# A decoder layer on one core: 24 matmuls that nothing reads are left out around the feed-forward products

## The chip, the cores and the metric

The kernel runs on one core of a Trainium2 chip. A core has a matrix engine (TensorE, PE in the profile, with its weight loads as PEld), VectorE (DVE), ScalarE (ACT), GpSimd (POOL) and DMA queues; each engine has its own instruction stream, and the streams meet only at semaphores. The metric is the device time of one execution in microseconds. The kernel before takes 385.61 us (median of 3 runs, 385.21 to 386.19).

## The reference, cut to what matters

A decoder layer in float32 over `x` of 8 x 256 x 128: self-attention of 16 heads of 64, cross-attention to 512 context rows, and a feed-forward layer with quantised products. Only the last part is touched:

```python
x = x + attn(layernorm(x))
x = x + cross_attn(ctx, ctx, layernorm(x))
x = x + ffn(layernorm(x))
def quant_linear(x, w, b):
    xq, s_in = quant_act_uint8(x)      # s_in = max over the WHOLE of x / 255
    wq, s_w = quant_weight_int8_perchannel(w)
    return einsum('btd,fd->btf', xq, wq) + quant_bias_int32(b, s_in, s_w)
h = relu(quant_linear(x, w1, b1))      # 2048 rows: 128 -> 512
return quant_linear(h, w2, b2)         # 2048 rows: 512 -> 128
```

Each of the two quantised layers needs one number, the largest element of its whole input, before its first product can be formed. So all of `h` must be there before the second layer starts.

## The kernel before, in words

Attention runs batch by batch in a loop and takes the span up to about 350 us. TensorE is the busiest engine there. Then the feed-forward layer is done once for all 2048 rows. Its activations stand transposed in `xrT`, 128 x 2048, and are taken in 4 chunks `n` of 512 columns; the hidden layer of 512 is 4 tiles `c` of 128. The order on each engine is written out by hand:

- TensorE, first layer (L726): 16 products `(n, c)`, each a 128x128 f16 weight tile against 512 columns, into the four banks `h_banks[c]` (score0, score1, turned_bank, q_bank1). Product `m` waits until eviction `m - 4` is done, since it takes over that bank (L725).
- ScalarE (L923): 16 evictions with bias and Relu from those banks into `h_sb`, which is part of the tensor `big`.
- VectorE (L1280): 16 reductions, one over each evicted tile, for the maximum. When all are done it forms `fmax`.
- TensorE (`spread_max(1, ...)`, L706): one f32 matmul that turns the 128 partial maxima of `fmax` onto every partition. VectorE then makes the scale out of it (L1239 to L1290).
- VectorE (L1297, 10 tiles) and ScalarE (L759, 6 tiles) quantise `h`; ahead of each tile's product TensorE waits for it (L748: 16 products, four accumulated in each of four banks). ScalarE evicts the four banks (L935), TensorE transposes them back after all 16 products (`turn_back`, L739, 16 transposes), VectorE adds the residual (L1306), and SyncE writes each of the 4 chunks of the output with a DMA of 256 KB.

`keep_warm(count, lhs, rhs, dst)` (L618) issues `count` matmuls into a bank that nothing reads. It is called at five places ahead of these products with the identity matrix, and those calls are not touched. Inside the first layer it is called at three places, with a weight tile and 512 columns of `x_qT` into `side_bank`: once after each product from `m = 4` on (12 matmuls), 8 after the last product, and 4 after `spread_max(1)`. None of these waits for a semaphore or sets one. `side_bank` is written again by the first transposes of `turn_back`.

Of the kernel before, what the change touches and what calls it, by code (L numbers as in the profile page):

```python
# [71 lines left out]
def decoder_layer(nc, x, ctx_in, norm_scale, wq, wk, wv, w_out, b_out, xWk, xWv, xbv, xWq, xbq,  # L72
# [41 lines left out]
    def wait(eng, sem, value):  # L114

        if isinstance(value, int) and value <= 0:
            return
        eng.wait_ge(sem, value)

    with ExitStack() as ctx:  # L120
        def sb(name, shape, dt=F32):
            return ctx.enter_context(nc.sbuf_tensor(name, shape, dt))

        def bank(name):
            return ctx.enter_context(nc.psum_tensor(name, [P, 512], F32))
# [95 lines left out]
        w1_qT = sb("w1_qT", [P, FT, P], F16)  # L221
# [15 lines left out]
        x_qT = xrT[:].bitcast(F16).rearrange("p (t half) -> p t half", half=2)[:, :, 0]  # L237
# [10 lines left out]
        side_bank = bank("side_bank")  # L248
# [201 lines left out]
        def _(pe):  # L450
# [165 lines left out]
            def keep_warm(count, lhs, rhs, dst):  # L616
                for _ in range(count):
                    nc.tensor.matmul(dst, lhs, rhs, start=True, stop=True)  # L618
# [84 lines left out]
            def spread_max(n, dst):  # L703

                pe.wait_ge(fmax_done, n + 1)
                nc.tensor.matmul(dst, fmax[:, n:n + 1].to_broadcast([P, P]), ident[:], start=True, stop=True  # L706
                                 ).then_inc(gmax_raw, 1)
# [11 lines left out]
            for n in range(CHUNKS):  # L719
                pe.wait_ge((xq_even, xq_odd)[n % 2], n // 2 + 1)  # L720
                for c in range(FT):
                    m = n * FT + c
                    if m == 2:
                        pe.wait_ge(xr_done, 5)
                    wait(pe, h_done, m - 3)  # L725
                    nc.tensor.matmul(h_banks[c][:], w1_qT[:, c, :], x_qT[:, n * 512:(n + 1) * 512],  # L726
                                     start=True, stop=True).then_inc(h_raw, 1)
                    if m >= 4:
                        keep_warm(1, w1_qT[:, c, :], x_qT[:, n * 512:(n + 1) * 512], side_bank[:])
            keep_warm(8, w1_qT[:, 0, :], x_qT[:, 0:512], side_bank[:])  # L730
            spread_max(1, acc_bank[:, 2 * P:3 * P])
            keep_warm(4, w1_qT[:, 0, :], x_qT[:, 0:512], side_bank[:])

            pe.wait_ge(h_done, CHUNKS * FT)

# [687 lines left out]
```

## Time and profile before

| | |
|---|---|
| device time, median of 3 runs | 385.61 us (385.21 to 386.19) |
| the profiled execution: device time, span | 386.2 us, 384.4 us |
| TensorE matmuls busy | 370.2 us (96% of the span) |
| VectorE, ScalarE, GpSimd busy | 325.8, 259.6, 174.3 us |
| first layer's products, from the first to the last one's start | 360.04 to 367.62 us |
| second layer's products | 373.43 to 378.34 us |
| transposes back | 378.18 to 380.09 us |

Times in the profile are counted from the span's start. Busy time of an engine is the time in which one of its instructions runs; matmuls overlap their neighbours, so a matmul's recorded duration is longer than its distance to the next one. The granted clock is TensorE's, as a share of 2.4 GHz: 1.00 is 2.4 GHz and 0.50 is 1.2 GHz. In a timeline a row stands for a run of like instructions: start, time from the first's start to the last's end, engine, line, operation, and the count behind the x; what stands in brackets is how long the engine was idle before and who released it.

### The profile page before, as it was taken

What the parts mean: (1) busy time and instruction counts of PE and PEld (TensorE: products, weight loads), DVE (VectorE), ACT (ScalarE), POOL (GpSimd) and SP (SyncE); (2) the same over time, 40 slices, a digit from 0 to 9 for tenths busy, and PEclk for the clock granted to TensorE, in tenths of its full rate; (3) what the DMA queues carried; (4) which work ended last, traced back from release to release, by engine and by line L of the source; (5) the groups of instructions that cost most, each with busy time, mean ns of one, the idle gap of its engine ahead of it and who ended that gap; (6) DMA issues with size and microseconds to landing.
All of it is one profiled execution on the core that took longest, in us unless ns stands there. A gap on an engine that the chain in (4) does not pass through costs nothing.

```text
span 384.4 us, 9135 instructions
## 1 busy us (share of the span) xinstructions
PE 370.2 (96%) x3034; PEld 288.4 (75%) x3034; DVE 325.8 (85%) x790; ACT 259.6 (68%) x812; POOL 174.3 (45%) x188
## 2 busy tenths in 40 slices
PE   8889999999999999999999999999999998999975
PEld 7768778778878877788777888787778876676422
DVE  3888879988998899879998899879987997876995
ACT  3867676766777567766677667756876668725664
POOL 2574435553555445545555454634555543521000
PEclk9999999999999999999999999999999999999999
DMA  7500000001000100001000100000000100000003
GB/s 231 166 15 2 2 0 2 3 3 41 2 1 3 42 0 0 0 0 41 0 0 0 41 0 0 0 30 10 0 0 0 27 2 2 2 2 0 2 0 109
DMA packets 7190, 7.50 MB, mean 20 GB/s; under 512 B 1280, under 2 KB 5120, under 8 KB 7168
## 3 DMA queue, kind: packets, MB, share of 16 engines
q1 hardware_dynamic: 6736, 6.69, 5.6%
q10 hardware_dynamic: 432, 0.52, 0.5%
q8 instruction: 13, 0.21, 0.2%
q14 instruction: 9, 0.07, 0.1%
HBM read 6.16 MB, written 1.05 MB: 19 GB/s over the span
## 4 chain that ended last, share of the span: by engine, by line
PE 81%; DVE 8%; ACT 7%; issue 3%; POOL 1%; POOLq 0%; DVEq 0%; ACTq 0%
PE o_bank L503 15%; PE turned_bank L494 14%; PE score L484 14%; PE acc_bank L510 7%; PE side_bank L453 4%; ACT prob L768 4%; PE q_bank L453 3%; PE q_bank L455 3%; PE q_bank L454 3%; PE side_bank L454 3%; PE side_bank L455 3%; PE side_bank L564 3%; DVE h_max L1280 2%; PE score L618 2%; PE side_bank L557 2%
## 5 line engine op out<-in xcount | busy, mean ns | idle before, releaser
L1324 POOL TENSOR_TENSOR prob<-prob,rinv 128x512 f32<-128x512 f32 x128 | 133.4, 1044 | 156.7 <-DVE rinv L955 156.4
L768 ACT ACTIVATE prob<-score,negmax 128x256 f32<-128x256 f32 x252 | 116.9, 473 | 36.2 <-DVE negmax L951 34.4
L958 DVE COPY pT<-turned_bank 128x512 f32<-128x512 f32 x124 | 84.1, 679 | 12.5 <-PE turned_bank L494 10.9
L951 DVE TENSOR_REDUCE negmax<-score 128x2 f32<-128x512 f32 x126 | 85.8, 682 | 3.4 <-PE score L484 1.1
L494 PE MATMUL turned_bank<-ident,prob 128*128 128x128 f32 x496 | 76.8, 277 | 0.3 <-DVE pT L958 0.2
L503 PE MATMUL o_bank<-pT,v_sb 128*64 128x256 f32 x504 | 68.3, 392 | 0.0
L494 PEld LDWEIGHTS turned_bank<-ident,prob 128*128 128x128 f32 x496 | 56.3, 141 | 9.1 <-issue 0.6
L768 ACT ACTIVATION_READ_ACCUMULATOR prob<-score,negmax 128x1 f32 x252 | 51.4, 204 | 0.0
L943 DVE TENSOR_TENSOR q_lo<-q_bank,q_hi 128x512 fp32r<-128x512 f32 x63 | 43.3, 689 | 6.8 <-ACT q_hi L759 4.9
L484 PE MATMUL score<-q_hi 64*128 64x256 f32 x252 | 42.3, 330 | 3.8 <-ACT prob L768 3.2
L503 PEld LDWEIGHTS o_bank<-pT,v_sb 128*64 128x64 f32 x504 | 30.5, 136 | 19.6 <-issue 9.2
L484 PEld LDWEIGHTS score<-q_hi 64*128 64x128 f32 x252 | 23.9, 184 | 25.8 <-issue 14.5
L453 PE MATMUL q_bank<-ht_hi,wqk_hi 128*128 128x256 f32 x124 | 40.2, 324 | 0.0
L510 PE MATMUL acc_bank<-wo_sb,oT 128*128 128x128 f32 x256 | 39.1, 276 | 0.0
L759 ACT ACTIVATE q_hi<-q_bank 128x512 fp32r<-128x512 f32 x63 | 38.1, 605 | 0.2
L759 ACT ACTIVATE v_sb<-side_bank 128x512 f32<-128x512 f32 x32 | 19.1, 598 | 26.6 <-PE side_bank L455 26.6
L510 PEld LDWEIGHTS acc_bank<-wo_sb,oT 128*128 128x128 f32 x256 | 34.7, 191 | 1.8 <-ACT oT L759 0.4
L484 PE MATMUL score<-q_lo,q_hi 64*128 64x256 f32 x252 | 35.9, 278 | 0.0
L484 PE MATMUL score<-q_hi,q_lo 64*128 64x256 f32 x252 | 35.8, 277 | 0.0
L455 PE MATMUL q_bank<-ht_hi,wqk_lo 128*128 128x256 f32 x124 | 34.9, 281 | 0.0
L454 PE MATMUL q_bank<-ht_lo,wqk_hi 128*128 128x256 f32 x124 | 34.8, 280 | 0.0
L759 ACT ACTIVATE oT<-o_bank 128x256 f32<-128x256 f32 x63 | 24.5, 388 | 6.2 <-PE o_bank L503 5.9
(249 smaller groups left out, 652.9 us busy)
## 6 DMA issues: line engine op xcount, KB each, us to landing
c_sb<-in_ctx_dram SPq DMA_DIRECT2D x8, 256.0 KB, 2.7
x_sb<-in_x_dram SPq DMA_DIRECT2D x8, 128.0 KB, 2.5
out_dram<-xn_all SPq DMA_DIRECT2D x4, 256.0 KB, 2.4
big<-in_L_attn_wk_dram ACTq DMA_DIRECT2D x2, 256.0 KB, 5.1
big<-in_L_attn_wq_dram SPq DMA_DIRECT2D x2, 256.0 KB, 5.6
big<-in_L_attn_wv_dram SPq DMA_DIRECT2D x2, 256.0 KB, 6.2
wo_sb<-in_L_attn_w_out_dram SPq DMA_DIRECT2D x1, 512.0 KB, 7.5
w_sb<-in_L_ffn_w_dram SPq DMA_DIRECT2D x2, 256.0 KB, 4.5
```

The source lines that it names most:

```text
L453: nc.tensor.matmul(dst, lhs_hi, rhs_hi, start=True, stop=False)
L454: nc.tensor.matmul(dst, lhs_hi, rhs_lo, start=False, stop=False)
L455: return nc.tensor.matmul(dst, lhs_lo, rhs_hi, start=False, stop=True)
L484: last = nc.tensor.matmul(banks[r][:, t * S:(t + 1) * S], query[rows, parity, 0, t * P:(t + 1) * P], key[rows, parity, 1, :], start=(n == ...
L494: last = nc.tensor.transpose(bank[:, kt * S + t * P:kt * S + (t + 1) * P], prob[:, slot, t, kt * P:(kt + 1) * P], ident[:])
L503: last = nc.tensor.matmul(bank[r * E:(r + 1) * E, 0:S], v_sb[:, vp, kt, h * E:(h + 1) * E], pT[:, slots[r], kt, :], start=(kt == 0), stop= ...
L510: last = nc.tensor.matmul(acc_bank[:, t * D:(t + 1) * D], oT[:, pair % 2, t * P:(t + 1) * P], wo_sb[:, pair, :], start=(pair == 0 and t == 0),
L759: return nc.scalar.activation(dst, src, ACT.Copy, **kw)
L768: last = nc.scalar.activation(prob[:, slot, t, :], banks[r][:, t * S:(t + 1) * S], ACT.Exp, bias=negmax[:, slot, t:t + 1], scale=1.0, accu ...
L951: nc.vector.tensor_reduce(negmax[:, slot], banks[r][:].rearrange("p (t k) -> p t k", k=S), X_AXIS, ALU.max, negate=True).then_inc(max_done, 1)
L958: nc.vector.tensor_copy(pT[:, slot].rearrange("p k q -> p (k q)"), bank[:]).then_inc(pT_done, 1)
L1324: nc.gpsimd.tensor_tensor(prob[:, slot], prob[:, slot], rinv[:, slot].unsqueeze(2).to_broadcast([P, QT, S]), ALU.mult).then_inc(prob_done, 1)
```

## The change

Three calls of `keep_warm` are deleted, 12 + 8 + 4 = 24 matmuls of 512 columns, each with its weight load. Everything else is as it was; the lines behind the deleted ones have numbers lower by 4.

```diff
                     nc.tensor.matmul(h_banks[c][:], w1_qT[:, c, :], x_qT[:, n * 512:(n + 1) * 512],
                                      start=True, stop=True).then_inc(h_raw, 1)
-                    if m >= 4:
-                        keep_warm(1, w1_qT[:, c, :], x_qT[:, n * 512:(n + 1) * 512], side_bank[:])
-            keep_warm(8, w1_qT[:, 0, :], x_qT[:, 0:512], side_bank[:])
             spread_max(1, acc_bank[:, 2 * P:3 * P])
-            keep_warm(4, w1_qT[:, 0, :], x_qT[:, 0:512], side_bank[:])
 
             pe.wait_ge(h_done, CHUNKS * FT)
```

On TensorE, in the first layer, one chunk of products (score0, score1, turned_bank and q_bank1 are the four banks of `h_banks`, xrT holds the quantised activations, w1_qT the weights):

```order
 L726 MATMUL q_bank1<-xrT,w1_qT 128x512
 L726 MATMUL score0<-xrT,w1_qT 128x512
-L618 MATMUL side_bank<-xrT,w1_qT 128x512
 L726 MATMUL score1<-xrT,w1_qT 128x512
-L618 MATMUL side_bank<-xrT,w1_qT 128x512
 L726 MATMUL turned_bank<-xrT,w1_qT 128x512
-L618 MATMUL side_bank<-xrT,w1_qT 128x512
 L726 MATMUL q_bank1<-xrT,w1_qT 128x512
-L618 MATMUL side_bank<-xrT,w1_qT 128x512
```

From the fifth product on, each product now stands next to the following one, and the wait of that one for its bank comes straight behind it.

On TensorE, between the two layers, before (fmax holds the partial maxima, big the quantised hidden layer; q_bank and o_bank receive the second layer's products):

```order
L726 MATMUL q_bank<-xrT,w_qT 128x512
L618 MATMUL side_bank<-xrT,w_qT 128x512 x9
L706 MATMUL acc_bank<-ident,fmax 128x128
L618 MATMUL side_bank<-xrT,w_qT 128x512 x4
L748 MATMUL q_bank<-big,w_qT 128x512 x4
L748 MATMUL o_bank<-big,w_qT 128x512 x4
```

and the same place in the changed kernel:

```order
L726 MATMUL q_bank<-xrT,w_qT 128x512
L706 MATMUL acc_bank<-ident,fmax 128x128
L744 MATMUL q_bank<-big,w_qT 128x512 x4
L744 MATMUL o_bank<-big,w_qT 128x512 x4
L744 MATMUL turned_bank<-big,w_qT 128x512 x4
```

The nine (the one behind the sixteenth product and the eight) and the four are gone, so that between the last product of the first layer and the first of the second TensorE has a single matmul, that of `spread_max(1)`.

## Rows read from the trace of the kernel before

**Rows 1.** The page's 40 slices: TensorE's granted clock in tenths.
```profile
PEclk9999999999999999999999999999999999999999
```

**Rows 2.** Chain of waits, 350 to 385 us: start, us, what.
```profile
361.24 8.70 DVE h_max L1280 x15
...
371.30 0.50 PE acc_bank L706 x2
...
378.82 1.89 DVE xn_all L1306 x3
380.70 0.60 DVEq L120
```

**Rows 3.** Timeline, first layer, 360 to 371 us, all engines.
```profile
360.52 1.26 ACT L923 ACTIVATE big<-score,b_col 128x512 f32<-128x512 f32 x2 [0.38 <-PE score L726]
...
361.24 9.59 DVE L1280 TENSOR_REDUCE h_max<-big 128x1 f32<-128x512 f32 x16
...
362.42 0.10 PEld L726 LDWEIGHTS turned_bank<-xrT,w_qT 128*128 128x128 f16 x1 [0.46 <-ACT big L923]
...
362.66 0.39 PE L618 MATMUL side_bank<-xrT,w_qT 128*128 128x512 f16 x1
...
369.08 0.80 ACT L923 ACTIVATE big<-q_bank,b_col 128x512 f32<-128x512 f32 x1
```

**Rows 4.** Timeline of PE from 367.6 to 373.5 us, between the layers.
```profile
367.62 0.40 PE L726 MATMUL q_bank<-xrT,w_qT 128*128 128x512 f16 x1
367.86 2.19 PE L618 MATMUL side_bank<-xrT,w_qT 128*128 128x512 f16 x9
371.30 0.49 PE L706 MATMUL acc_bank<-ident,fmax 128*128 128x128 f32 x2 [1.25 <-DVE fmax L1287]
371.62 1.07 PE L618 MATMUL side_bank<-xrT,w_qT 128*128 128x512 f16 x4
373.43 0.39 PE L748 MATMUL q_bank<-big,w_qT 128*128 128x512 f16 x1 [0.74 <-DVE big L1297]
```

**Rows 5.** Timeline, second layer, 373 to 381 us.
```profile
374.58 2.86 DVE L1297 TENSOR_SCALAR big<-big,h_scale 128x512 f32<-128x512 f32 x7
...
375.11 0.10 PEld L748 LDWEIGHTS o_bank<-big,w_qT 128*128 128x128 f16 x1 [0.86 <-DVE big L1297]
...
377.16 1.18 PE L748 MATMUL q_bank<-big,w_qT 128*128 128x512 f16 x4
...
378.62 1.04 PE L739 MATMUL score<-ident,xrT 128*128 128x128 f32 x8
...
379.49 0.60 PE L739 MATMUL acc_bank<-ident,xrT 128*128 128x128 f32 x4
...
380.62 0.68 DVE L1306 TENSOR_TENSOR xn_all<-acc_bank,x_all 128x512 f32<-128x512 f32 x1
```

**Rows 6.** Windows: length, busy of PE, PEld, DVE, ACT, POOL, clock, DMA.
```profile
371.30:373.40 2.10, 1.39 (x6) 0.60 (x6) 1.47 (x7) 0.60 (x1) 0.00 (x0) 1.00 0.00 0
...
380.10:383.00 2.90, 0.00 (x0) 0.00 (x0) 1.20 (x3) 0.00 (x0) 0.00 (x0) 1.00 0.88 297
383.00:384.40 1.40, 0.00 (x0) 0.00 (x0) 0.00 (x0) 0.00 (x0) 0.00 (x0) 0.50 0.38 135
```

**Rows 7.** Line 618 alone, 1.6 to 7.1 us: minimum/median/maximum ns.
```profile
L618 PEld LDWEIGHTS score<-ident x26: 289/333/338, 1.6 to 6.9; 128*128 128x128 f32 x26
L618 PE MATMUL score<-ident x25: 421/421/580, 1.6 to 6.9; 128*128 128x128 f32 x25
```

**Rows 8.** Line 618 in the whole span: minimum/median/maximum ns.
```profile
L618 PEld LDWEIGHTS side_bank<-ident x28: 190/192/192, 355.4 to 359.6; 128*128 128x128 f32 x28
L618 PE MATMUL side_bank<-ident x28: 275/275/275, 355.5 to 359.7; 128*128 128x128 f32 x28
```

**Rows 9.** Timeline, 352 to 384.4 us: identity matmuls at 355 us.
```profile
355.49 2.40 PE L618 MATMUL side_bank<-ident 128*128 128x128 f32 x20
```

**Rows 10.** Timeline of PE, 1.6 to 8.4 us, and the window 1.6 to 7.5.
```profile
1.61 6.66 PE L618 MATMUL score<-ident 128*128 128x128 f32 x32 [1.61 <-POOL ident L1369]
...
1.60:7.50 5.90, 5.89 (x27) 5.90 (x28) 2.69 (x9) 2.54 (x3) 1.93 (x3) 1.00 0.81 250
```

**Rows 11.** The page's list of DMA issues: the output.
```profile
out_dram<-xn_all SPq DMA_DIRECT2D x4, 256.0 KB, 2.4
```

## The prediction

> **What bounds the kernel now.** I read the slices of the page first, for the clock, then the chain of waits over the last 35 us, the timeline there engine by engine, and windows cut where TensorE starts and stops. The slices show 9 throughout, a granted clock of 2.4 GHz up to the end [rows 1]. The chain shows who holds the time around the change. Through the first feed-forward layer it is VectorE, 15 maxima in a row [rows 2]: the 16 start every 0.59 us ((9.59 - 0.68) / 15), while ScalarE's 16 evictions start every 0.571 us ((369.08 - 360.52) / 15) and stay ahead [rows 3]. TensorE is not in the chain there: its weight load for a product sat idle 0.46 us for ScalarE to give back the bank [rows 3]. Then comes a short relay, last maximum, `fmax`, the spreading matmul of TensorE at 371.30, the scale, the first quantised tiles, and then the second layer's products, the transposes and the additions, with TensorE in the chain [rows 2]. After the last addition only the output's DMAs are left.
>
> **What goes, and what it gives back directly.** 24 matmuls of 512 columns at one per 0.225 us ((2.19 - 0.39) / 8, nine in a row) are 5.4 us of TensorE [rows 4]. None of that is on the path:
> - The 12 beside the products stand in time in which TensorE would wait for a bank; the next product starts when ScalarE is done, not when the side matmul is [rows 3]. Gain 0.
> - The 8 behind the last product (nine with its own) end at 370.05; the spreading matmul starts at 371.30, after 1.25 us of idling for `fmax` [rows 4]. Gain 0.
> - The 4 behind it end at 372.69, and the first product of the second layer starts at 373.43 after 0.74 us of idling for a quantised tile [rows 4]. Gain 0.
> - No semaphore hangs on them, so no other engine's waits change.
>
> What could be gained is less contention. ScalarE's evictions grow from about 0.63 to 0.80 us in the record while their distance stays, and VectorE reads only `big` there, so the 0.59 us step of the maxima is the pace to be sped up. Its bounds are 0 and the step falling to ScalarE's 0.571: 15 x 0.023 = 0.35 us. I take 0, since VectorE and TensorE share no tile there.
>
> **What they cover.** With them TensorE's idle stretches between the layers are 1.25 and 0.74 us, and the clock stays at 1.00 [rows 4, 6]. Without them the last product of the first layer ends at 368.0, the spreading matmul comes at 371.30 and runs 0.5 us, and nothing follows till 373.43: 3.3 us idle, one matmul, 1.6 us idle. The nearest row is the end of the program: TensorE's last transpose ends at 380.09, the clock is 1.00 from 380.10 to 383.00 and 0.50 from 383.00 on [rows 5, 6]. So 2.9 us after TensorE stopped the chip took the clock to 1.2 GHz. By the same delay it would fall at 368.0 + 2.9 = 370.9, ahead of the spreading matmul, and the second layer would begin at 1.2 GHz. Even if it held until 371.3, one matmul of half a microsecond in a stretch of 5.4 us is little to keep it up. The Trainium skill, "TensorE: Matmul & The Clock Gate", What's actually happening, says the same from the other side: the slow clock is the default and activity is what lifts it, with no levels but the two. By that rule the side matmuls are work after all; the trace's drop at 383.00 agrees.
>
> **What the slow clock costs.** Its price in matmuls is read where the same form runs at both. The identity matmuls at the start of the program take 421 ns, their weight loads 333 [rows 7]; those at 355 to 360 us take 275 and 192 [rows 8]. The page gives 1.00 for the start too (window 1.60 to 7.50 [rows 10]), but the durations show the lower level: the distance from one to the next is 0.221 us at the start (25 of them from 1.6 to 6.9, 5.3 / 24) against 0.112 us at 355 us ((2.40 - 0.28) / 19) [rows 7, 9]. The ratio is 1.97, so a 512-column product goes from 0.225 to an estimated 0.443 us.
>
> - First layer: if the clock fell already there, a product would take 0.443 us in a step of 0.57, and it has three evictions' time (1.7 us) before ScalarE wants it. Cost 0.
> - Spreading matmul: two passes. Each is 0.146 us longer in latency (421 - 275), overlapping, and the second starts 0.109 us later (0.221 - 0.112): 0.26 us, right on the path. The other end is 0, if the clock falls later than 371.3. I take 0.26, because 370.9 is earlier.
> - Second layer: 16 products now take 373.43 to 378.34, 4.91 us, because they wait for tiles. The last tile of VectorE is ready at 374.58 + 2.86 = 377.44 [rows 5]. At 0.443 us each the products no longer wait for any tile (the fifth would start at 373.43 + 4 x 0.443 = 375.20, and its tile let it start at 375.11 [rows 5]), so TensorE becomes the bound. If the clock is low for t microseconds from the first product on, t / 0.443 products are done in it, the rest follow at 0.225, and the last one's drain is 0.17: t + (16 - t / 0.443) x 0.225 + 0.17 = 3.77 + 0.492 t. Over the 4.91 of now that is 0.492 t - 1.14.
>
> The disputed number is t, how long TensorE must work before the clock comes back. The trace has one such return: from the first matmul at 1.61 until about 7.5 us all are slow [rows 7, 10], 5.9 us of almost unbroken work. The other row on how fast the chip answers is the 2.9 us of the fall [rows 6]. With t = 5.9 the cost is 1.76 us, with 2.9 it is 0.29 us. Neither is nearer, since the one started from a cold chip with a wait for x in the middle and the other is a fall, so I take the middle, t = 4.4, and 0.492 x 4.4 - 1.14 = 1.02 us.
>
> **Where the delay ends up.** The first chunk's transposes follow the last product, the first addition follows them, and each DMA follows an addition, so a delay of the last product reaches the end whole. The additions (0.60 us apart) and the four DMAs keep their pace; the output's transfer, 256 KB four times [rows 11], is busy until about 383 [rows 6]. Sum: 0 + 0.26 + 1.02 = 1.3 us, on the profiled execution 386.2 + 1.3 = 387.5 us. That execution stands 0.6 us above the median of the runs, so the forecast on the median is 385.61 + 1.3 = 386.9 us.
>
> **Rivals.**
> - *The clock never falls* (not slower). The place is 368.0 to 373.4. For it: the fall at 383.00 came after total silence, while here a matmul interrupts at 371.30, and 1.25 and 0.74 us of idling did nothing. Against it: 3.3 us is longer than 2.9. It decides if the silent stretch that the chip bears is over 3.3 us; then the cost is 0 and the time 385.6 us.
> - *The clock falls and does not come back before the end.* The products then take 16 x 0.443 + 0.17 = 7.26 us, 2.35 more. The 16 transposes come at a distance of 0.110 us now ((1.04 - 0.27) / 7 [rows 5]) and of 0.22 then, another 1.75. The last addition starts at 380.62 where its tile was ready at 380.09 [rows 5], so 0.53 of that is absorbed, and the last DMA waits behind the others some 0.5 us now, which goes too. With 0.26 for the spreading matmul the cost is 0.26 + 2.35 + 1.75 - 0.53 - 0.5 = 3.3 us, time 388.9 us. For it: the return took 5.9 us in the one case seen, and the slow products last 7.3. Against it: 5.9 is less than 7.3. The Trainium skill, same page, Part 4: PE-mode transpose, says that the full clock does not engage for transposes. The transposes of this trace run at 1.00 with 0.110 us between them, so they do not lose a clock that is up; whether they could raise one no row here shows, and if not, a clock still low at the last product stays low, which is this rival.
> - *Less contention*: the maxima speed up and the clock stays. 385.61 - 0.35 = 385.3 us, the floor.
>
> **How the numbers follow.** Clock falls and returns during the second layer 0.72, with 385.9 to 387.6 us as its own range (0.29 to 1.76, with 0 to 0.26); never falls 0.13; never returns 0.10; less contention 0.05. A measurement of this kernel tells about 0.3%, 1.16 us, from no change. In the likeliest case that needs 0.492 t - 1.14 + 0.26 over 1.16, t over 4.15, some 58% of 2.9 to 5.9: 0.42. With the 0.10 of no return, slower has 0.52; faster by that much has 0.02, since no mechanism gives over 0.35 us; the rest, 0.46, is the same. The range is 385.5 to 388.3 us: it takes in the unchanged case and a t somewhat past 5.9, and leaves out most of the no-return case.
>
> **What the profile after would show.** The fall: a granted clock of 0.50 in a window between 371 and 377 us, and the 9s of the slices broken near the end. The spreading matmul: its two passes at 0.7 to 0.75 us instead of 0.49. The second layer: its first products 0.44 us apart, the weight loads no longer waiting for VectorE, later ones 0.22 apart, with the change of distance 3 to 6 us behind the first product. First layer: the maxima still 0.59 us apart and over by 370.9. The forecast is wrong if the clock is 1.00 in all windows up to the transposes' end (then no change), if the transposes are 0.22 us apart (then +3.3), or if the first layer gets longer or shorter by over 0.4 us.

## The result, and the profile after

The changed kernel takes 387.82 us (median of 7 runs, 386.3 to 388.3) beside 385.44 us before (385.12 to 386.19). The ratio is 1.0053, 95% interval 1.0036 to 1.0070: about 2.0 us slower (1.4 to 2.7). The two medians lie 2.4 us apart; the ratio goes by all the executions of both, and the sums below are held against its 2.0. Two more sets of runs of the same kernel gave 1.0048 (1.0035 to 1.0061) and 1.0036 (1.0021 to 1.0051).

The page's slices of the changed kernel, which answer to [rows 1]:

```profile
PE   8889999999999999999999999999999998999855
...
PEclk9999999999999999999999999999999999999958
```

Windows of the changed kernel, cut at what TensorE does; columns as in [rows 6]:

```profile
360.00:365.00 5.00, 3.55 (x12) 0.86 (x9) 4.92 (x11) 4.89 (x9) 0.00 (x0) 1.00 0.01 3
365.00:370.90 5.90, 2.72 (x6) 0.45 (x5) 5.75 (x12) 4.47 (x8) 0.00 (x0) 0.50 0.00 0
370.90:373.30 2.40, 0.77 (x2) 0.49 (x3) 1.49 (x7) 0.61 (x1) 0.00 (x0) 0.50 0.00 0
373.30:378.60 5.30, 5.28 (x13) 1.72 (x14) 3.88 (x12) 4.51 (x8) 0.00 (x0) 0.50 0.00 0
378.70:381.30 2.60, 2.60 (x20) 2.00 (x18) 1.23 (x3) 1.50 (x2) 0.00 (x0) 1.00 0.00 0
```

The clock stands at 2.4 GHz up to 365.0, in the middle of the first layer, at 1.2 GHz from there to between 378.6 and 378.7, and at 2.4 GHz again for the transposes. Second layer and the matmul ahead of it, on TensorE, timeline of the changed kernel, where [rows 4, 5] stood:

```profile
367.21 0.61 PE L726 MATMUL q_bank<-xrT,w_qT 128*128 128x512 f16 x1
370.88 0.80 PE L706 MATMUL acc_bank<-ident,fmax 128*128 128x128 f32 x2 [3.06 <-DVE fmax L1283]
373.32 1.86 PE L744 MATMUL q_bank<-big,w_qT 128*128 128x512 f16 x4 [1.65 <-DVE big L1293]
375.00 1.89 PE L744 MATMUL o_bank<-big,w_qT 128*128 128x512 f16 x4
376.69 1.91 PE L744 MATMUL turned_bank<-big,w_qT 128*128 128x512 f16 x4
378.40 1.20 PE L744 MATMUL q_bank<-big,w_qT 128*128 128x512 f16 x4
...
379.87 1.04 PE L735 MATMUL score<-ident,xrT 128*128 128x128 f32 x8
```

Four products take 1.69 us from group to group, 0.42 us each, and nothing stands in brackets behind the second and third group: the tiles are there, TensorE is the bound. The last group is at 2.4 GHz for the most part, 1.20 us against 1.18 in [rows 5]. The spreading matmul takes 0.80 us, not 0.49.

The chain of waits, changed kernel (answers to [rows 2]):

```profile
360.83 8.71 DVE h_max L1276 x15
...
370.88 0.81 PE acc_bank L706 x2
...
373.32 1.86 PE q_bank L744 x4
375.19 1.71 PE o_bank L744 x4
376.89 1.71 PE turned_bank L744 x4
...
380.07 1.89 DVE xn_all L1302 x3
381.95 0.60 DVEq L120
```

The maxima take what they took (8.71 us against 8.70). Three groups of products stand in the chain in a row, 1.86, 1.71 and 1.71 us.

**Where the time went.** Counted from the first product of the first layer (360.04 before, 359.62 after) to the span's end, the kernel before takes 24.36 us and the changed one 26.04, so +1.68 in this pair. Three parts make it up. From the first product to the spreading matmul it is 11.26 us in both, a difference of 0.00. The spreading matmul gives 0.31. The 16 products take 6.28 us (373.32 to 379.60) against 4.91, which gives 1.37. Everything behind is shifted. The profiled span is only 1.3 us longer since the changed kernel reached the first layer 0.42 us earlier, for a reason that has nothing to do with the change (last section).

### The profile page after: what moved, and what is told of

Same layout as the page of the kernel before. It is cut to its first block, busy times and chain, and to the rows that moved or that the text cites. A ratio compares the mean times of both kernels' runs of the same rounds, so it can differ in the third digit from the quotient of the medians.

```text
span 385.7 us, 9087 instructions
## 1 busy us (share of the span) xinstructions
PE 367.8 (95%) x3010; PEld 287.5 (75%) x3010; DVE 325.8 (84%) x790; ACT 260.2 (67%) x812; POOL 174.6 (45%) x188
## 4 chain that ended last, share of the span: by engine, by line
PE 81%; DVE 7%; ACT 7%; issue 3%; POOL 1%; POOLq 0%; DVEq 0%; ACTq 0%
PE o_bank L503 15%; PE turned_bank L494 14%; PE score L484 14%; PE acc_bank L510 7%; PE side_bank L453 4%; ACT prob L764 4%; PE q_bank L453 3%; PE q_bank L455 3%; PE q_bank L454 3%; PE side_bank L454 3%; PE side_bank L455 3%; PE side_bank L564 3%; DVE h_max L1276 2%; PE side_bank L557 2%; PE score L618 2%
```

## Experiments

All ratios are to the kernel before on the same chip, with 95% intervals. In the diffs, `...` is left out. "Low" is the stretch at 1.2 GHz. Where it begins or ends is worked out from the mean clock of the window in which that lies: 0.81 over 3 us means 1.14 us of low.

**Which of the three groups matters.** Four kernels, each the one before with a part left out.

e1_no12:
```diff
-                    if m >= 4:
-                        keep_warm(1, w1_qT[:, c, :], ...)
```


> Left out: only the 12 side matmuls beside the first layer's products; the 8 behind them and the 4 behind the spreading matmul stay. Theory (the clock pays): as in the changed kernel the clock falls in the middle of the first layer, since its products alone leave TensorE idle over half the time; the 8 and the 4 then run slow and nearly without a gap from 367.8 us on, so TensorE is back at full clock some 5 us later, by about 373, and the second layer is little slowed. The 8 at 0.44 us each end at about 371.4, up to 0.5 us after fmax is ready, which delays the spreading matmul. Expected +0.5 us over the kernel before (0 to +1.2). Rival (only the silence between the layers matters): no fall, +0.0 us. Rival (the time of the change is not the clock's but lies in where the instructions stand): about half of the +2.0 us, since half of them are gone.

Measured: 0.9991 (0.9982 to 1.0001). The profiled execution has the clock at 1.00 through both layers. In it the products alone did not bring the clock down before the 8 came, and the 8 ran at full speed and delayed nothing.

```profile
365.00:370.00 5.00, 3.67 (x13) 1.07 (x12) 5.00 (x10) 4.45 (x8) 0.00 (x0) 1.00 0.02 3
370.00:373.00 3.00, 1.39 (x6) 0.63 (x7) 2.25 (x10) 0.63 (x1) 0.00 (x0) 1.00 0.00 0
```

My expectation of +0.5 us missed; the 12 are worth nothing while the others stay. Neither theory that gave a cost holds for this group. The clock need not stay up in every execution: four of the eleven have a mean clock of 0.993 or 0.994, against 0.997 or more in all 35 of the kernel before beside them, so 2 to 3 us more of low, at a place that no trace shows. Their times, 385.96 to 386.44 us, are within those of the kernel before.

e2_no8:
```diff
-            keep_warm(8, w1_qT[:, 0, :], x_qT[:, 0:512], side_bank[:])
```


> Left out: only the 8 side matmuls behind the first layer's last product. TensorE is then idle for 3.2 us ahead of the spreading matmul, with the first layer and the 4 behind it as before. Theory: if 3.2 us of silence alone brings the clock down, it falls near 371 and the 4 side matmuls already count towards its return, so the second layer is slow for some 3 us: +0.3 to +0.8 us. Rival (the fall needs the sparse first layer too): the clock stays at 1.00, +0.0 us. Rival (instructions, not clock): a third of +2.0 us, +0.7, with the clock at 1.00.

Measured: 1.0000 (0.9992 to 1.0009). The clock did fall, ahead of the second layer, and was back by 375.6, so low for 2.4 us of it; that lies inside the waits for tiles and costs nothing. Windows of this kernel:

```profile
370.00:373.00 3.00, 1.51 (x6) 0.60 (x6) 2.25 (x10) 0.43 (x1) 0.00 (x0) 0.86 0.00 0
373.00:376.00 3.00, 2.80 (x8) 0.92 (x9) 2.86 (x11) 3.00 (x6) 0.00 (x0) 0.57 0.00 0
```

My +0.3 to +0.8 us was too much, since it left out that slack. The rival that the fall needs a sparse first layer is out, and so is the one that a share of the instructions is a share of the time (+0.7 us): a third of them costs nothing.

e3_no4:
```diff
-            keep_warm(4, w1_qT[:, 0, :], x_qT[:, 0:512], side_bank[:])
```


> Left out: only the 4 side matmuls behind the spreading matmul. TensorE is idle 1.25 us ahead of it and then 1.7 us behind it. Theory: shorter than any silence that brought the clock down, so the clock stays at 1.00 and the time is that of the kernel before, +0.0 us (-0.3 to +0.3). Rival (instructions, not clock): +0.3 us.

Measured: 1.0015 (1.0005 to 1.0026), +0.6 us. The expectation missed: the clock fell at about 372.9, inside the 1.65 us behind the spreading matmul, though I had held that stretch too short, and stayed low until 376.3. Windows of this kernel:

```profile
371.90:372.80 0.90, 0.00 (x0) 0.00 (x0) 0.80 (x5) 0.00 (x0) 0.00 (x0) 1.00 0.00 0
372.90:376.20 3.30, 2.73 (x7) 0.87 (x8) 3.16 (x11) 3.30 (x6) 0.00 (x0) 0.50 0.00 0
376.30:379.00 2.70, 2.70 (x16) 1.51 (x15) 1.18 (x3) 2.70 (x5) 0.00 (x0) 1.00 0.00 0
```

e4_only12 leaves out both the 8 and the 4.

> Left out: the 8 and the 4, so that the first layer runs exactly as before with its 12 side matmuls, and the silence between the layers is that of the changed kernel. Theory: the clock stays at 1.00 through the first layer, falls between 371 and 373.4, and the return has to be earned by the second layer's own products, 3.4 to 6 us of them: +0.8 to +2.0 us, like the changed kernel. Rival (the sparse first layer is what brings it down): +0.0 us. If the time is well below that of the changed kernel although the clock falls, what the first layer adds is the slow spreading matmul, 0.3 us.

Measured: 1.0025 (1.0014 to 1.0036), +1.0 us. With the first layer just as before, the clock falls in the silence behind it (low from about 370.4) and is back at 377.3, 4.8 us into the second layer. So the sparse first layer isn't needed for the loss; this is about half of it, by the silence alone.

**What is left when only one group stays.**

e5_only4 leaves out the 12 and the 8.

> Left out: the 12 beside the first layer's products and the 8 behind them; only the 4 behind the spreading matmul stay. Theory (the second layer pays for each microsecond at 1.2 GHz that it starts with): the clock falls as in the changed kernel, the spreading matmul is slow (+0.3 us), but TensorE's unbroken work begins at 371.7 with the 4 instead of at 373.4, so the clock comes back some 1.7 us earlier and 0.49 us is saved for each of these: +1.2 us over the kernel before (0.6 to 1.8), against some +2.0 for the changed kernel on the same chip. Rival (side matmuls behind the spreading matmul are too few to count): +2.0 us, as the changed kernel.

Measured: 0.9999 (0.9990 to 1.0008). 20 of the 24 are gone and nothing is lost. The clock fell, but it came back 0.5 us after the second layer's first product, much earlier than either theory had it. TensorE's timeline and the windows of this kernel:

```profile
370.14 0.80 PE L706 MATMUL acc_bank<-ident,fmax 128*128 128x128 f32 x2 [3.28 <-DVE fmax L1284]
370.73 1.91 PE L618 MATMUL side_bank<-xrT,w_qT 128*128 128x512 f16 x4
372.59 1.33 PE L745 MATMUL q_bank<-big,w_qT 128*128 128x512 f16 x4
374.27 1.25 PE L745 MATMUL o_bank<-big,w_qT 128*128 128x512 f16 x4 [0.35 <-DVE big L1294]
```
```profile
366.90:369.70 2.80, 0.00 (x0) 0.00 (x0) 2.77 (x5) 1.81 (x4) 0.00 (x0) 1.00 0.00 0
369.80:373.10 3.30, 2.96 (x8) 1.18 (x8) 2.27 (x10) 1.15 (x2) 0.00 (x0) 0.50 0.00 0
373.20:377.30 4.10, 3.75 (x15) 1.17 (x15) 3.25 (x11) 4.10 (x8) 0.00 (x0) 1.00 0.00 0
```

The spreading matmul is slow (0.80), the 4 run slow in time in which TensorE would have stood still, and the products have their waits for tiles again (0.35).

e6_only8 leaves out the 12 and the 4.

> Left out: the 12 beside the first layer's products and the 4 behind the spreading matmul; only the 8 behind the last product stay. Theory: the 8 in a row come before the clock can fall, as in the kernel that left out the 12 alone and stood at 1.00, and what is left is the 1.65 us of silence before the second layer, which cost +0.6 us where only the 4 were left out: +0.6 us (0.2 to 1.2), spreading matmul at full clock. Rival (the sparse first layer brings the clock down before the 8 come): spreading matmul slow and delayed, +1.0 to +2.0 us.

Measured: 1.0028 (1.0018 to 1.0039), +1.1 us, at the upper end of what the theory gave. The spreading matmul is fast (0.49 us at 370.07), so the 8 did keep the clock up to it. The fall came at about 373.5, when the second layer's products had been running since 372.21.

```profile
370.00:373.00 3.00, 1.28 (x5) 0.58 (x6) 2.29 (x10) 1.42 (x3) 0.00 (x0) 1.00 0.00 0
373.00:376.00 3.00, 2.65 (x7) 0.72 (x8) 2.88 (x9) 3.00 (x6) 0.00 (x0) 0.59 0.00 0
```

So the clock can fall when work has already begun again. It was back at 376.9, after 3.4 us, as long a stretch as in e3_no4, yet the 16 products took 5.98 us (372.21 to 378.19) against 5.08 there: the stretch lies later, where less of it falls into waits for tiles.

**The price by itself.** e7_double slows the second layer's products without touching the clock:
```diff
+                    nc.tensor.matmul(acc_bank[:], w2_qT[:, c, :], h_q[:, c, n * 512:(n + 1) * 512], start=True, stop=True)
                     last = nc.tensor.matmul(yT_banks[n][:], w2_qT[:, c, :], h_q[:, c, n * 512:(n + 1) * 512],
```


> The kernel before with all its side matmuls, and one more matmul of the same tile, into a bank that nobody reads, ahead of each of the 16 products of the second layer. Nothing of the clock changes; it measures by itself what it costs when a product takes 0.45 us there instead of 0.225. Theory: TensorE becomes the bound, the 16 products take 16 x 0.45 + 0.17 = 7.4 us instead of 4.9, and the whole of it reaches the end: +2.4 us (2.1 to 2.6), at a clock of 1.00. Rival (the waits for the quantised tiles or the output's DMAs hide it): +0.5 us or less, and then the slow clock in the second layer can't be what the changed kernel pays.

Measured: 1.0050 (1.0037 to 1.0063), 1.9 us (1.4 to 2.4), the expected 2.4 at the interval's end. In the trace the second layer takes 7.41 us (372.75 to 380.16) instead of 4.91, and from the first layer's first product (359.36) to the end it is 26.84 us against 24.36: +2.5 us, all of it arrives. The clock:

```profile
372.80:380.00 7.20, 7.20 (x33) 3.06 (x34) 3.81 (x12) 5.32 (x9) 0.00 (x0) 1.00 0.00 0
```

So twice the time for each product costs, at full clock, about what the changed kernel loses, and a delay of the second layer reaches the end whole.

**The changed kernel again.** e8_again and e12_third are the changed kernel unaltered.

> The changed kernel once more, beside the three others on the same chip. Theory: +2.0 us over the kernel before (1.4 to 2.7), and its clock record again shows 1.2 GHz from the first layer or the silence behind it until some 4 to 6 us into the second. If the record is another one (a fall later, a return later), its time must differ by 0.49 us for each microsecond of slow second layer and 0.3 us for a slow spreading matmul.

> The changed kernel a third time, for its clock record. Of the two profiled so far the slow clock lasted 5.34 and 4.03 us into the second layer, which by 0.47 us each and 0.31 us for the spreading matmul makes +1.7 and +1.1 us counted from the first layer's first product, while the middle of all its executions is +2.0 us. Theory: the length differs by execution, and a profiled one at 387.5 us or over must show a low clock for 5.5 us or more of the second layer, up to all of it (16 products at 0.425 us, +2.4 us in all); one at 386.3 us must show 4 us or less, or a clock that is back ahead of the spreading matmul. Rival (something beside the clock adds half a microsecond): a high time with 4 us or less.

Measured: 1.0048 and 1.0036. The profiled executions have the clock low from 369.8 to 376.7 and from 370.3 to 377.1, not from 365.0 on. Their windows:

```profile
376.00:379.00 3.00, 3.00 (x17) 1.77 (x16) 0.87 (x3) 2.57 (x4) 0.00 (x0) 0.89 0.00 0
```
```profile
370.00:373.00 3.00, 1.28 (x4) 0.54 (x4) 2.19 (x10) 1.30 (x3) 0.00 (x0) 0.55 0.00 0
...
376.00:379.00 3.00, 3.00 (x16) 1.67 (x15) 0.51 (x2) 2.22 (x4) 0.00 (x0) 0.81 0.00 0
```

The expectation for the third was wrong in one number: its profiled execution took 386.2 us with 4.8 us of low clock, not 4 or less. I had left out that executions also differ in when they reach the feed-forward layer: this one at 358.81, against 360.04 of the profile before. Counted from there it is +1.2 us. The times of the ten runs fall in two groups, 386.0 to 386.5 and 387.3 to 387.9; those of the first set are 386.3 (two) and 387.5 to 388.3 (five), and the second set has one between, 387.02. None of the three profiled executions is among the dearest: they took 387.46, 386.19 and 386.2 us. Every execution has a mean clock on record, though. All 22 of the changed kernel have 0.991 or less, those of the kernel before 0.994 or more. Seven, of 387.64 to 387.98 us, have 0.987, some 10 us of low in all, which no profiled one of this kernel has; three of the cheapest, 385.96 to 386.31 us, have 0.981, the most low of all. So the length of the low alone does not set the time.

**Two variations of the 4.**

e9_fill:
```diff
-                    if m >= 4:
-                        keep_warm(1, w1_qT[:, c, :], ...)
-            keep_warm(8, ...)
+            keep_warm(12, ...)
             spread_max(1, acc_bank[:, 2 * P:3 * P])
-            keep_warm(4, ...)
+            keep_warm(6, ...)
```


> The 12 beside the first layer's products are left out, and the silences between the layers are filled instead: 12 side matmuls behind the last product (they end near 370.6, still ahead of fmax at 371.25) and 6 behind the spreading matmul (they end near 373.1, ahead of the first tile). If the kernel before pays nothing for the clock, this can't be faster than it: 385.6 us, -0.1 us to +0.2 us, clock 1.00 through the second layer. Rival (some executions of the kernel before still fall in their 1.25 and 0.74 us of silence): faster by 0.2 to 0.5 us and with less spread between executions.

Measured: 1.0006 (0.9997 to 1.0015), 385.1 to 386.4 us, as wide as before. This is as expected, and the rival is out. Nothing is to be had by filling the silences further: the kernel before pays nothing there, and no version here beats it clear of noise.

e10_ident:
```diff
-            keep_warm(4, w1_qT[:, 0, :], x_qT[:, 0:512], side_bank[:])
+            keep_warm(4, ident[:], ident[:], side_bank[:, 0:P])
```
with the 12 and the 8 left out.

> All 24 left out, but 4 f32 matmuls of the identity with itself, 128 columns, two passes each, stand behind the spreading matmul in place of the 4 of 512 columns. Their array time is nearly the same: 8 passes at 0.112 us, 0.9 us. Theory (it is TensorE's activity in that silence that counts, not these operands): as with the 4 of 512 columns, +0.0 us (-0.4 to +0.5). Rival (the 4 f16 matmuls help in another way, by their operands or their weights): +2.0 us, as the changed kernel.

Measured: 1.0015 (1.0006 to 1.0024), +0.6 us, most of the 2 us saved by matmuls of other operands, type and shape. In its profiled execution the clock was back at 374.0, and the second layer took 4.92 us (372.45 to 377.37), so nothing was lost there. That execution was the fastest of the twelve (385.23 us), so what costs the others the 0.6 us, just over the upper end of what I expected, stays open.

e11_only2 is the same with `keep_warm(2, w1_qT...)`.

> All left out but 2 side matmuls behind the spreading matmul, half of what sufficed. Theory (activity is weighed, in part by chance of where the silence lies): between the 4 (+0.0) and none (+2.0): +0.8 us (0.2 to 1.6), with a clock that in some executions is low for most of the second layer. Rival (any matmul there keeps the clock, since only unbroken silence counts): +0.0 us.

Measured: 1.0046 (1.0028 to 1.0064), +1.8 us, more than I expected: 2 save nothing that can be told from the changed kernel's loss, where 4 save all. The clock came back at 377.0, 3.9 us into the second layer. The rival that any matmul there suffices is out.

**Most of them by one rule.** The table has the profiled executions whose clock was low from the second layer's first product on, and the kernel before. In it t is how long it stayed low from there, in us; then come the time of the 16 products, and what a product pace of 0.4225 us in the low stretch gives, 3.77 + 0.467 t, with the form that the prediction derived. The slope is 1 - 0.225 / 0.4225.

| kernel | t | 16 products, measured | by the rule | ratio |
|---|---|---|---|---|
| before | 0 | 4.91 | waits for tiles, 4.91 | |
| e5_only4 | 0.5 | 4.91 | under 4.91 | 0.9999 |
| e2_no8 | 2.4 | 4.91 | 4.89 | 1.0000 |
| e3_no4 | 2.8 | 5.08 | 5.08 | 1.0015 |
| e11_only2 | 3.9 | 5.59 | 5.59 | 1.0046 |
| e8_again | 4.0 | 5.66 | 5.64 | 1.0048 |
| e12_third | 4.8 | 6.00 | 6.01 | 1.0036 |
| e4_only12 | 4.8 | 6.02 | 6.01 | 1.0025 |
| changed | 5.3 | 6.28 | 6.24 | 1.0053 |

The ratio is that of all executions, t that of the profiled one, so the last column need not follow the first row by row. The rule does not cover e6_only8, whose low stretch began inside the layer, and e10_ident (t = 1.5, 4.92 us) kept its waits for tiles.

## Why the prediction was right, point by point

The forecast on the median was 386.9 us, +1.3, within 385.5 to 388.3; the measured median is 387.82, and the ratio gives +2.0. The mechanism was right: the clock falls, the second layer becomes bound by TensorE, and the delay reaches the end. That the number came as near as it did is in part luck, since the moment of the fall and the length t both turned out to differ from execution to execution.

- *The removed matmuls give nothing back directly.* Right. From the first layer's first product to the spreading matmul it is 11.26 us in both traces, and the maxima keep their pace. The less-contention case is out: e1_no12, which leaves out just the 12 beside the products, also has 11.26 us (359.61 to 370.87).
- *The clock falls.* Right that it does; the moment was not. The prediction put it at 370.9, from the 2.9 us of [rows 6]; the three profiled executions have 365.0, 369.8 and 370.3. One is inside the first layer, where it cost nothing, as the prediction had it for that case. In the other two it came 2.9 and 3.5 us after the first layer's last product had ended, much as the prediction reasoned. But length of silence alone does not settle it: in the changed kernel's profile the clock fell while the first layer's products ran, in e3_no4 within the 1.65 us of silence, and in e6_only8 after the second layer had begun.
- *Spreading matmul +0.26 us.* Measured 0.31 (0.80 against 0.49) where the clock is low all through it, a little over the 0.7 to 0.75 that the prediction gave as the sign, and 0.12 to 0.13 in e4_only12 and e12_third, where it fell in its course.
- *Price of a slow product, 0.443 us.* Measured 0.42. The form 3.77 + 0.492 t was right and its slope is 0.467. The bound shifts to TensorE and the delay reaches the end, which e7_double showed by itself.
- *t = 4.4 us.* This is the term that was mis-sized for the middle of the executions, though not for each: 5.3, 4.0 and 4.8 in three profiles, inside the 2.9 to 5.9 that were taken from the rows. With 0.31, 0.31 and 0.13 for the spreading matmul these come to +1.7, +1.1 and +1.2 us from the first layer on; the sum of the prediction was 1.3. The middle was luck: the upper row, 5.9 us, is that of one execution. The opening matmuls of e8_again were back at full clock at about 4.4 us, 2.8 us after the first (last section), and the 2.9 us are of a fall. The three comparisons gave +2.0, +1.9 and +1.4 us. Some executions must be costlier than the three profiled ones; the dearest, 388.3 us, is 2.9 above the median before and 1.9 above the slowest execution of the kernel before on record (386.42). I have no trace of such a one, and that they are those with t near 7 (all 16 products slow: 6.93 us, +2.0, and 0.31) is an estimate, not shown; nor is it shown that nothing beside the clock adds to them.
- *No return before the end*: in none of the profiled executions; the transposes are 0.110 us apart in the changed kernel too ((1.04 - 0.27) / 7). Whether transposes can bring the clock up stays open, since it was up each time before they began.
- *Never falls*: out, by three profiles of three and the mean clock of all 22 executions.

What the prediction did not see is how unequal the three groups are. The 4 behind the spreading matmul suffice: with them alone it is 0.9999, without them alone 1.0015, and with neither them nor the 8 1.0025. They lie directly ahead of the work that needs the clock, in time in which TensorE idles anyway. The plainest pair is e5_only4 and e8_again: the clock fell at 369.7 and 369.8, the second layer began at 372.6 in both, and the clock was back at 373.1 with the 4 and at 376.7 without them.

## What to carry to other kernels

A matmul that nothing reads can be the cheapest thing on the path: price it by what the next dense stage of TensorE costs at half clock, and ask of that stage whether it has slack (here the first 2.4 us of low clock from its start on were free and each further one cost 0.47; in e6_only8 the low stretch began inside the stage, and 3.4 us of it cost 1.07). Put such matmuls right ahead of the dense stage, in the wait for its first operand; 4 there did what 24 spread over both layers did, and 2 did not. When such a group is judged, take away each part alone as well as all, since the parts are not additive: 12 + 8 cost 0.0 us, 4 alone 0.6, all 2.0.

## What the runs showed of the hardware that I had not expected

- The same program has its clock lowered at different places in different executions: at 365.0, 369.8 and 370.3 us. The low stretches that began ahead of the transposes lasted 3.4 us in five profiles (e2_no8, e3_no4, e5_only4, e6_only8, e10_ident), 6.8 us in four (e4_only12, e8_again, e11_only2, e12_third) and 13.7 us in one (the changed kernel's first), and no other length occurred. In e6_only8 the fall came 1.3 us after the second layer's first product.
- Much of the spread of times, which the kernel before has too (385.05 to 386.42 beside e1_no12), is there before the changed part begins: in the 14 profiles the first layer's first product starts anywhere from 358.81 to 360.08. The opening matmuls run at 1.2 GHz for a time that differs. The same 32 passes, timelines of the kernel before [rows 10], of the changed one and of e8_again:

```profile
1.61 6.21 PE L618 MATMUL score<-ident 128*128 128x128 f32 x32 [1.61 <-POOL ident L1365]
```
```profile
1.61 5.26 PE L618 MATMUL score<-ident 128*128 128x128 f32 x32 [1.61 <-POOL ident L1365]
```

  At 5.8 us they are slow in the kernel before and fast in e8_again (line 618 in the window 5.8 to 6.0: minimum/median/maximum ns):

```profile
L618 PE MATMUL score<-ident x3: 421/421/421, 5.4 to 5.8; 128*128 128x128 f32 x3
```
```profile
L618 PE MATMUL score<-ident x4: 275/275/275, 5.6 to 5.9; 128*128 128x128 f32 x4
```

  They take 6.66, 6.21 and 5.26 us, and the first layer's first product starts at 360.04, 359.62 and 358.94. Two single executions can thus differ by 1 us with no cause in the code; counting from a landmark behind the start takes that out. e1_no12 doesn't fit so well (5.29 us, yet 359.61), so this is not all of it.
- The page's clock of 1.00 for the first microseconds is no evidence; the durations of the matmuls there, 421 against 275 ns [rows 7, 8], are.
